# Window attention and a two-of-eight expert layer on one core: written-out strips, gate rows spread by pairs of experts, and a new order of work

## What is computed

```python
x = x + attention(ln_c(x))          # 8x8 windows, 4 heads, bias_table[rel_index], softmax, w_proj, b_proj
t = tokens(x)                       # one token per pixel, 64 channels
h = ln_t(t)
probs = softmax(h @ router_w + router_b)
top_p, top_i = top_k(probs, 2)      # two of eight experts
top_p = top_p / sum(top_p)
expert_out = einsum("bnd,edc->bnec", h, expert_w) + expert_b
t = t + sum_k top_p[k] * expert_out[top_i[k]]
```

## Time and profile before

| | us |
|---|---|
| median of 3 executions | 1319.18 |
| lowest and highest | 1318.9, 1325.99 |
| the profiled execution | 1319.76 |
| its span, first to last instruction | 1317.8 |

### The profile page before, as it was taken

One profiled execution on the slowest core, in us unless ns is written; L12 is line 12 of the kernel. 1 busy time (PEld: TensorE's weight loads), 2 busy tenths in 40 slices (PEclk: granted clock), 3 DMA queues, 4 the chain that ended last, 5 costly groups with the idle time before them and its releaser, 6 DMA issues.

```text
span 1317.8 us, 41226 instructions
## 1 busy us (share of the span) xinstructions
PE 1108.7 (84%) x16678; PEld 578.2 (44%) x16678; DVE 920.3 (70%) x1398; ACT 707.6 (54%) x1153; POOL 439.8 (33%) x359
## 2 busy tenths in 40 slices
PE   4688998888899979987998879899799889988754
PEld 2344444444444434443544435444344444444311
DVE  3247787778777767885778757777677877776642
ACT  1366565555565646654665546665466566555410
POOL 1003234433443233343234424432343344233342
PEclk9999899999999989998999989999899999998877
DMA  3216676777766658877576777776588777755676
GB/s 127 65 42 155 147 183 174 179 199 189 197 159 173 174 143 199 198 195 188 123 184 171 180 183 190 169 177 173 136 199 200 194 188 162 172 146 143 153 174 169
DMA packets 91494, 219.85 MB, mean 167 GB/s; under 512 B 17728, under 2 KB 30656, under 8 KB 91200
## 3 DMA queue, kind: packets, MB, share of 16 engines
q1 hardware_dynamic: 91328, 217.32, 66.3%
HBM read 177.15 MB, written 23.33 MB: 152 GB/s over the span
## 4 chain that ended last, share of the span: by engine, by line
PE 44%; DMA 26%; issue 11%; SPq 9%; DVE 6%; ACT 2%; POOL 1%; POOLq 0%; DVEq 0%; ACTq 0%
DMA gz<-gates_dram 22%; PE bank L620 14%; SPq L347 8%; PE bank L501 6%; PE bank L462 5%; PE bank L534 5%; PE bank L551 3%; PE bank L558 3%; DMA gates_dram<-gsb 3%; PE bank L489 3%; PE bank L516 2%; DVE mx L1005 2%; DVE probs L1012 2%; PE bank L588 2%; DVE gz L1026 1%
## 5 line engine op out<-in xcount | busy, mean ns | idle before, releaser
L1026 DVE TENSOR_TENSOR gz<-gz,tt 128x1024 f32<-128x1024 f32 x160 | 301.6, 1889 | 127.3 <-DMA gz<-gates_dram 127.2
L620 PE MATMUL bank<-gz,wex 64*64 64x512 f32 x2048 | 276.8, 648 | 47.7 <-issue 33.2
L915 POOL TENSOR_TENSOR gz<-gz,tt 128x1024 f32<-128x1024 f32 x96 | 250.4, 2619 | 23.9 <-DMA gz<-gates_dram 23.9
L889 POOL TENSOR_TENSOR tt<-prj,xs 128x512 f32<-128x512 f32 x64 | 106.3, 1681 | 437.1 <-ACT prj L779 437.1
L762 ACT ACTIVATE pt<-bank 128x512 f32<-128x512 f32 x256 | 150.5, 588 | 106.4 <-PE bank L534 106.4
L1005 DVE TENSOR_REDUCE mx<-bank 128x16 f32<-128x1024 f32 x128 | 155.6, 1216 | 58.4 <-PE bank L501 58.4
L1012 DVE TENSOR_TENSOR probs<-bank,mx 128x1024 f32<-128x1024 f32 x128 | 156.7, 1224 | 43.3 <-PE bank L534 34.3
L501 PE MATMUL bank<-km,qs 32*64 32x128 f32 x4096 | 177.7, 289 | 3.4 <-issue 0.5
L534 PE MATMUL bank<-cst,probs 128*128 128x128 f32 x1024 | 173.3, 293 | 5.1 <-ACT pt L762 5.1
L501 PEld LDWEIGHTS bank<-km,qs 32*64 32x64 f32 x4096 | 113.4, 136 | 111.4 <-issue 100.1
L534 PEld LDWEIGHTS bank<-cst,probs 128*128 128x128 f32 x1024 | 110.7, 144 | 114.3 <-issue 48.0
(11 more groups left out here) (95 smaller groups left out, 1259.8 us busy)
## 6 DMA issues: line engine op xcount, KB each, us to landing
gz<-gates_dram SPq DMA_DIRECT2D x512, 256.0 KB, 7.9
xs<-in_x SPq DMA_DIRECT2D x32, 512.0 KB, 10.6
rstd<-std_dram SPq DMA_DIRECT2D x64, 256.0 KB, 4.0
tx<-tt SPq DMA_DIRECT2D x128, 128.0 KB, 9.2
out<-ob SPq DMA_DIRECT2D x128, 128.0 KB, 9.1
gates_dram<-gsb SPq DMA_DIRECT2D x32, 192.0 KB, 2.1
grow<-gates_dram SPq DMA_DIRECT2D x192, 32.0 KB
gz<-in_rel SPq DMA_DIRECT2D x1, 2048.0 KB, 8.8
```

What stands on the lines that cost most here:

```text
L620: last = mm(bank[64 * x:64 * x + 64, Y_BANK + a, :], wex[64 * a:64 * a + 64, e, :], gz[64 * a:64 * a + 64, e, x * CH:(x + 1) * CH], start= ...
L915: tt_(gz[:, e, :], gz[:, e, :], tt[s.buf(4)][:, :], op=ALU.mult).then_inc(z_pool, 1)
L1026: tt_(gz[:, e, :], gz[:, e, :], tt[s.buf(4)][:, :], op=ALU.mult).then_inc(z_dve, 1)
```

## The change

The steps are written out for all 38, without a loop (`U`, `Fori`, the register counts and the `sem_inc` calls on `waited` and `sp_waited` go). `gz` becomes a ring of six places, each for a pair of experts (`GZ_RING = 6`); a transfer of `spread_gates` now brings two rows of 1024 gates to 64 partitions, 512 KB, and there are 8 for a strip where there were 16. The order of calls changes on all five engines. Some calls change their step: `square`, `channel_sums` and `variance` run for `s[0]`, one step earlier than before; `transposes` 0 and 1 and `row_max` 2 of a strip run one step earlier; `residual(…, 0)` too; `gated` 0 and 2 one step later; `move_v`, `experts` 7, `expert_bias_rows` and `finish` one step later. `lnv`, `cand` and `L2` are no longer buffers of their own. No instruction of the computation is added or taken away.

```diff
-        gz = sb("gz", [P, E, LT])
+        gz = sb("gz", [P, GZ_RING, 2, LT])
...
         ROUNDS = {
-            0: [("stats", 1, var_done, 1), ("lgT", 4, L_ready, 2), ("Q", 2, q_ready, 1), ("K", 2, k_ready, 2),
-                ("gT", 4, gsb_ready, 1), ("V", 2, v_ready, 2), ("proj", 3, prj_ready, 1)],
...
+            0: [("lgT", 4, L_ready, 2), ("K", 2, k_ready, 2), ("Q", 2, q_ready, 1), ("stats", 0, var_done, 1),
+                ("gT", 4, gsb_ready, 1), ("proj", 3, prj_ready, 1), ("V", 2, v_ready, 2)],
...
+            def pair(self, e):
+
+                return divmod(4 * self.c + e // 2, GZ_RING)
...
-            with nc.Fori(0, n, engines=(run.engine,)) as r:
-                for v in range(U):
-                    run(Step(lo + v, r, True))
...
+        def stepped(f):
+            for c in range(STRIPS + LAST_STAGE):
+                f(Step(c))
+            return f
...
-            def spread_gates(s, e):
-
-                if e == 0:
+            def spread_gates(s, q):
+
+                if q == 0:
                     sp.wait_ge(gates_written, s.count(16, 16))
-                    sp.sem_inc(sp_waited, 1)
-                wait(sp, e_done, s.count(E, e + 1, lag=1))
+
+                wait(sp, e_done, 2 * (s.count(4, q) - GZ_RING + 1))
+                k = s.count(4, q) % GZ_RING
                 for a in range(2):
-                    sp.dma_start(gz[64 * a:64 * a + 64, e, :],
-                                 gates_dram[s.buf(4), 0, E * a + e, :].partition_broadcast(64)
-                                 ).then_inc(gz_loaded[e], 16)
+                    sp.dma_start(gz[64 * a:64 * a + 64, k, :, :].rearrange("p e t -> p (e t)"),
+                                 gates_dram[s.buf(4), 0, E * a + 2 * q:E * a + 2 * q + 2, :].rearrange(
+                                     "e t -> (e t)").partition_broadcast(64)).then_inc(gz_loaded[k], 16)
...
+            @stepped
             def _(st):
                 s = st.strips()
                 if s[5].on:
-                    spread_gates(s[5], 6)
-                    spread_gates(s[5], 7)
+                    spread_gates(s[5], 2)
+                    spread_gates(s[5], 3)
                 if s[6].on:
                     store(s[6])
                 if s[0].on:
                     load(s[0])
-                if s[4].on:
-                    swap_tokens(s[4])
                 if s[5].on:
                     load_gate_rows(s[5])
                 if s[1].on:
                     write_std(s[1])
                     spread_std(s[1])
                 if s[4].on:
+                    swap_tokens(s[4])
                     write_gates(s[4])
                     spread_gates(s[4], 0)
                     spread_gates(s[4], 1)
-                    spread_gates(s[4], 2)
-                    spread_gates(s[4], 3)
-                    spread_gates(s[4], 4)
-                    spread_gates(s[4], 5)
```

More of the change, by code:

```diff
@@ L20 @@
 PARTS = 3
-U = 4
 BIG = 3.0e38
@@ L645, in _ @@
                 if s[3].on:
-                    values(s[3], 1)
+                    scores_right(s[3], 3)
+                if s[5].on:
+                    experts(s[5], 0)
+                if s[2].on:
+                    keys(st, s[2])
                 if s[5].on:
                     experts(s[5], 1)
+                    experts(s[5], 2)
+                if s[3].on:
+                    transposes(s[3], 4)
+                    values(s[3], 2)
+                    values(s[3], 3)
                 if s[2].on:
@@ L695, in _ @@
                 if s[2].on:
-                    transposes(s[2], 0)
                     scores_right(s[2], 2)
+                if s[5].on:
+                    experts(s[5], 6)
+                if s[2].on:
+                    value_rows(st, s[2])
                 if st.c == 0:
@@ L930, in _ @@
                     gated(s[5], 7)
+                if s[3].on:
+                    residual(s[3], 0)
         @block.vector
@@ L1123, in _ @@
                     token_statistics(s[4])
+                if s[5].on:
+                    gated(s[5], 3)
                 if s[3].on:
+                    row_max(s[3], 3)
+                    normalise(s[3], 0)
                     shift(s[3], 3)
-                if s[1].on:
-                    guard_variance(s[1])
                 if s[4].on:
@@ L1133, in _ @@
                     pick_two(s[4])
-                    gates(s[4])
-                if s[3].on:
-                    normalise(s[3], 0)
                 if s[2].on:
@@ L1139, in _ @@
                     shift(s[2], 0)
+                if s[4].on:
+                    gates(s[4])
                 if s[3].on:
                     normalise(s[3], 1)
+                if s[5].on:
+                    gated(s[5], 5)
+                if s[0].on:
+                    variance(s[0])
+                if s[2].on:
+                    row_max(s[2], 1)
+                if s[3].on:
+                    normalise(s[3], 2)
+                if s[2].on:
+                    shift(s[2], 1)
+                if s[0].on:
+                    guard_variance(s[0])
+                if s[3].on:
+                    normalise(s[3], 3)
                 if s[5].on:
```

244 lines of the change are left out of this document (101 added, 143 removed).

## The result

The changed kernel takes 1264.02 us (median of 4 executions, 1261.08 to 1264.95) beside 1321.96 for the kernel before in the same comparison: a ratio of 0.956, 95% interval 0.952 to 0.959. The forecast was 1213 with a range of 1165 to 1265, so the direction is right and the time lies at the upper edge of the range, 1 us inside it and 51 us above the forecast. The profiled execution took 1263.9, its span 1262.0.

A forecast was written before the change was run, and what follows sets the result against it. The prediction took a circle of spread, multiply, route, spread (36.1 us), not PE, to bound the kernel. It summed 112.9 - 5 + 31 x 34.7 - 5 + 32.1 = 1210.7, plus 2.0 around it: 1213 us, range 1165 to 1265.

The forecast's parts named there:

- The loop: Steps in the loop: written out, they should cost what the steps behind it cost, 27 us less, or 32.
- The landing of pairs: Spread of gates: pair 0 (experts 0, 1) lands at 8.4 us after SP's first issue, pair 1 at 12.9.
- G: Start of SP's first issue of the spread of a strip's gates, from which times in a period are counted.
- pair 1 lands with the rest: Spread: eight transfers share the DMA engines, pair 1 lands at G + 22.1; 42.2 us a period, 1450 in all; chance 0.04.
- The binding circle: Per period: the path through the load, 34.4 us, is longer than that of the gates, 33.0, and PE's 32.
- So the rows come no faster.: Spread by pairs: SP saves about 5 us of issues, hidden because DMA is full at 229 GB/s.
- circle of the load: Spread, load landing at G + 24.6, square, channel sums, other PE work, transposed gates, next G: 34.4 us with additional waits.
- the clock falls in every period: Rival on PE: a 2.4 us wait halves the clock each period; 36.2 us a period, 1259 in all; chance 0.20.
- the term of +0.3 a period: PE's clock: lowered after waits in one period in six, where every period would cost 1.8 us; 34.4 becomes 34.7.
- The load isn't late: Rival: the burst runs 8% or more faster, the gates' circle binds at 33.0 us; 1165 in all; chance 0.25.
- The circle of the gates: Spread to pair 1 12.9, DVE's multiply and routing to `gates` 13.6, on to next G 6.5: 33.0 us a period.
- The ends: Fill 112.9 less 5 at the bias matmuls, drain 32.1 unchanged, last periods without a load 5 less in all.

The follow-up runs named there:

- the kernel where it alone binds: Changed kernel with the next strip's load issued ahead of gate pairs 2 and 3, and gates spread by 256 KB transfers: 1229.62 us, ratio 0.932.

## Why the prediction was right, and where it was not

**The loop.** Priced at 27 us, it was 22.7 by medians (12 to 27). Right, slightly high. One reading was wrong: of the five waits in the earlier trace rows, 33.2 us is the total and 8.3 the longest. Four, of 8.1 to 8.3, lie between the five turns, and the fifth is 0.3.

**The landing of pairs.** G + 8.4 and G + 12.9 were predicted, G + 8.3 and G + 13.1 measured. The rival by which pair 1 lands with the rest, at 22.1, is out.

**The binding circle.** That the load would take the gates' place as the last to come was right: 18% of the chain, ACT waiting in 25 periods, PE ahead of the channel sums. Its sum of 34.4 was met in the kernel with 256 KB transfers, at 1213 us, where small misses cancel: the load landed 0.5 early and the rest took 0.5 longer.

**"So the rows come no faster."** This is the step that failed. It took 229 GB/s over unchanged, and for the load it asked only whether larger transfers might be faster. The larger transfers are slower, 221 GB/s, and the load, behind them all in the queue, lands later. The pieces of the circle of the load, read from the timelines of every period that has a load (27, means in us):

| | priced | changed kernel | with 256 KB |
|---|---|---|---|
| G to the landing of the load | 24.6 | 25.65 | 24.07 |
| landing to channel sums | 1.04 | 1.41 | 1.36 |
| channel sums to transposed gates | 5.2 | 5.58 | 5.59 |
| transposed gates to the next G | 3.35 | 3.57 | 3.49 |
| additional waits, clock | 0.2, 0.3 | in the rows above | in the rows above |
| period | 34.7 | 36.21 | 34.51 |

Of the 1.70 between the two kernels the landing is 1.58 (by medians, 25.5 and 24.3, it is 1.2: one period of the 256 KB kernel has it at 20.6). Of the 1.5 that the forecast was short, the landing is 1.05 and all else together 0.45. Only the transfers differ between 1264.0 and 1213.5, and that is 50 us of the 51 missed. The two rules of the Trainium skill's "SBUF — State Buffer" that the prediction weighed were both about this. The one of "The DMA setup-cost knee" (the largest single transfer) points the wrong way here. That of "Door 1: The DMA port swizzle" (64 partitions, some 218 GB/s) is met by 218 and 221, though 256 KB transfers to alternating halves exceed it with 234.

**The clock.** The rival "the clock falls in every period" named 1259, close to what came, but it isn't what happened. In the changed kernel the clock falls between channel sums and transposed gates in 5 periods of 27, about the one in six that was taken. There the stretch takes 6.4 to 7.8 where it is else some 5.3, so the term of +0.3 a period was about right. In the mean the stretch is no longer than in the 256 KB kernel, where it happens once. The range ended at 1265 because this rival was to lie in it. That the measured 1264 lies in it for another reason is luck.

**"The load isn't late", 1165.** Moving the load early did not give this: 1262 and 1230. The circle of the gates beneath it was priced at 33.0, is at least 35.4 in the changed kernel and 35.1 in the kernel where it alone binds. There 2.0 us are routing operations and 1.0 `gb`, both stretched beside the other engine's multiply; the other pieces came out 0.9 shorter together. The prediction took 1.35 off because POOL has nothing to multiply between pairs 0 and 2, and did not ask what POOL's multiply of expert 4 would then lie beside. So two terms were off, and the second would have shown itself only once the first was mended.

**The ends.** The fill is 112.7, not 107.9. The gain at the bias matmuls came: the first keys start at 33.3 instead of 39.9. But the write of the first gates is issued only 2.1 us earlier, at 108.71, and takes 4.0 us instead of 2.07, as in the other kernels with the new order (3.6 to 4.0); why was not looked into. The drain is 32.9 for 32.1. The last two periods, 32.9 and 30.9, are short by 8 together, 5 was predicted.

So the sum, 107.9 + 31 x 34.7 - 5 + 32.1, missed by 4.8 in the fill, 45.6 in the periods and 0.8 in the drain. The change is good for its order and its straight code; its transfers by pairs cost it 50 us, nearly as much as the 58 it gained. With single experts' transfers, the load ahead and one multiply moved it takes 1192 us.

## What to carry to other kernels

Before transfers are merged, ask who waits for the last byte of the queue, and bound the new rate from below as well as from above: fewer, larger transfers shortened SP's issues, which no run shows to matter, and slowed the data that the period hung on. When two circles are of nearly the same length, an edit to either shows nothing or a loss; change both together and read the two by two table. When one piece looks too long in one period, take its mean over all periods before it is blamed. When work of GpSimd is moved or comes late, look at which small operations of VectorE it will then lie beside.

## What the runs showed of the hardware

- Queued transfers of 512 KB to 64 partitions ran at 220 to 222 GB/s (medians), with rows of 4 or of 8 KB; 256 KB to alternating halves at 234 and 235, or 240 with a load over 128 partitions among them. DMA's busy share read 1.02 or 1.03 in both, so a full share doesn't mean that the rate can't be better.
- A 128x128 operation of VectorE of 0.29 us took 2.38 beside GpSimd's 128x1024 multiply of 2.38, and GpSimd's of 0.41 took 1.39 beside VectorE's multiply of 1.3. With the multiplies apart both were back at 0.29 and 0.41.
- In one period of the kernel with 256 KB transfers DMA moved 300 GB/s over the 16 us from G + 2 on, 340 over 8 us of it, at a share of 1.00 and 0.96; the load landed at G + 20.6. This stays unexplained.
- A transfer to 128 partitions whose source has an outermost dimension of 2 moved 52 GB/s at a share of 0.13 of 16 engines.
